# Root product moved into the maxima, transposes of a chunk issued earlier, ScalarE's register loads and two input loads moved

## What is computed

```python
h = maximum(layernorm(x), 0)
# layer 0: mean over incoming edges, applied twice
n1 = segment_sum(h[src], dst) / max(deg, 1)
n2 = segment_sum(n1[src], dst) / max(deg, 1)
x = x + 0.5 * n1 + 0.5 * n2
h = maximum(layernorm(x), 0)
# layer 1: two convolutions with a maximum over incoming edges
def conv(X, Wm, We, Wr, b):
    agg = segment_max(X[src] @ Wm + edge_attr @ We, dst)   # 0 where a node has no edge
    return agg + X @ Wr + b
c1 = leaky_relu(conv(h,  W1_msg, W1_edge, W1_root, b1))
c2 = leaky_relu(conv(c1, W2_msg, W2_edge, W2_root, b2))
return x + c2
```

## Time and profile before

| | us |
|---|---|
| median of 3 runs | 8090.3 (8090.01 to 8094.53) |
| profiled execution | 8085.28 |
| its span | 8083.5 |
| GpSimd busy (74%) | 5982.4 |
| TensorE busy (62%) | 5040.0 |
| VectorE busy (41%) | 3320.8 |
| ScalarE busy (18%) | 1432.1 |
| mean granted clock of TensorE | 0.700 of 2.4 GHz |

### The profile page before, as it was taken

How to read it: one execution, slowest core, us unless ns; L and a number is a source line. 1 busy time by engine, 2 the same in 40 slices (tenths; PEclk the granted TensorE clock), 3 DMA queues, 4 the chain that set the end, 5 groups by cost and what they waited for, 6 DMA issues and landing times.

```text
span 8083.5 us, 153739 instructions
## 1 busy us (share of the span) xinstructions
PE 5040.0 (62%) x25651; PEld 3760.0 (47%) x25651; DVE 3320.8 (41%) x7074; ACT 1432.1 (18%) x4686; POOL 5982.4 (74%) x6411
## 2 busy tenths in 40 slices
PE   3444454445344444444677878777787787878777
PEld 2333333334333333333555655555575565555556
DVE  5444444445433333333533433333343343333335
ACT  2000000001000000000422333323242232333323
POOL 6777777776777777777677777777766777777777
PEclk9965555556555555555677888888787888888888
DMA  3111111111211111111144444344323444444443
GB/s 92 42 42 41 42 41 41 41 41 47 57 41 42 41 41 41 41 41 41 40 94 93 98 92 97 89 96 93 92 69 91 98 93 92 98 93 92 95 95 80
DMA packets 337343, 553.28 MB, mean 68 GB/s; under 512 B 212648, under 2 KB 212648, under 8 KB 311848
## 3 DMA queue, kind: packets, MB, share of 16 engines
q0 software_dynamic: 196096, 301.60, 18.2%
q1 hardware_dynamic: 129796, 243.57, 11.8%
q10 hardware_dynamic: 10788, 2.16, 0.2%
HBM read 521.97 MB, written 24.87 MB: 68 GB/s over the span
## 4 chain that ended last, share of the span: by engine, by line
POOL 53%; issue 21%; SPq 10%; PE 10%; DMA 3%; DVE 2%; ACT 1%; ACTq 0%; DVEq 0%; POOLq 0%
POOL rows L443 53%; SPq L288 5%; SPq L311 4%; PE ps L673 3%; PE ps L671 3%; DMA rows<-table,src_sb 2%; PE ps L695 2%; SPq L294 1%; PE ps L684 1%; PE ps L757 1%; PE ps L770 1%; ACT arena L488 0%; DMA arena<-in_eat 0%; DMA table<-arena 0%; PE ps L652 0%
## 5 line engine op out<-in xcount | busy, mean ns | idle before, releaser
L443 POOL DMA_INDIRECT rows<-table,src_sb x6128 | 5788.3, 945 | 1957.9 <-issue 1847.0
L652 PE MATMUL ps<-arena,rows 128*98 128x128 f32 (+1 forms) x6088 | 1518.7, 430 | 2103.7 <-DMA rows<-table,src_sb 1362.9
L652 PEld LDWEIGHTS ps<-arena,rows 128*98 128x98 f32 (+1 forms) x6088 | 1263.9, 277 | 2381.1 <-DVE comp L882 2011.2
L897 DVE TENSOR_TENSOR_SCAN arena<-arena,ps 96x512 f32<-96x512 f32 x782 | 997.5, 1276 | 2424.3 <-PE ps L673 2419.5
L882 DVE TENSOR_TENSOR comp<-comp,ps 98x128 f32 (+1 forms) x3128 | 895.6, 286 | 2165.8 <-PE ps L652 1851.1
L671 PE MATMUL ps<-arena,we 32*96 32x512 f32 x1564 | 1001.2, 724 | 797.1 <-DMA rows<-table,src_sb 471.6
L673 PEld LDWEIGHTS ps<-ident,rows 128*96 128x96 f32 x6168 | 825.9, 188 | 718.8 <-issue 718.8
L865 DVE TENSOR_TENSOR arena<-ps,meta 128x512 f32<-128x512 f32 x1564 | 1051.0, 672 | 29.7 <-issue 26.1
L673 PE MATMUL ps<-ident,rows 128*96 128x128 f32 x6168 | 1017.0, 317 | 0.0
L513 ACT COPY comp<-ps 96x128 f32 x3128 | 818.9, 262 | 1067.2 <-PE ps L695 806.2
L695 PE MATMUL ps<-arena 128*96 128x128 f32 x6256 | 946.0, 302 | 1.3 <-ACT arena L504 1.3
(11 more groups left out here) (98 smaller groups left out, 1065.0 us busy)
## 6 DMA issues: line engine op xcount, KB each, us to landing
side<-table SPq DMA_DIRECT2D x10240, 0.4 KB
arena<-flags SPq DMA_DIRECT2D x194, 768.0 KB
rows<-table,src_sb POOLq DMA_INDIRECT x6128
side<-table ACTq DMA_DIRECT2D x5120, 0.4 KB
arena<-in_eat SPq DMA_DIRECT2D x194, 256.0 KB
table<-arena SPq DMA_DIRECT2D x56, 336.0 KB, 2.8
out<-xs SPq DMA_DIRECT2D x13, 336.0 KB
tail<-table SPq DMA_DIRECT2D x256, 0.4 KB
```

The lines of the kernel that those rows point to most:

```text
L443: pool.indirect_dma_start(rows[:, g % RING, j, 0:D], None, tables[r][:, :], bass.IndirectOffsetOnAxis(src_sb[:, c:c + 1], 0)).then_inc(lan ...
L652: m = pe.matmul(ps[0:w, at + k * P:at + (k + 1) * P], got[k][:, 0:w], hot[:, j % HOTS, k, :], start=True, stop=True)
L897: dve.tensor_tensor_scan(run[:, slot % SCANS], fe[0:D, slot // UNIT, q * W:(q + 1) * W], ps[0:D, ROWS + slot % 2 * BANK:ROWS + slot % 2 * ...
```

## The change

- In rounds 2 and 3 `own_part` is new on ScalarE and TensorE. In each sweep of 8 groups two tiles of `root`, which now holds the nodes' features themselves, are copied to `h_tile`, transposed, copied to `h_turned_sb` (its row 96 is ones), multiplied with the root weights and bias, and copied back over the tile in `root`.
- In rounds 1 and 2 the features go straight into `root` (L488 and L1050 write there), the product has 96 columns, and the copy L595 and the last chunk's second product L778 are gone. The ones row of `hT` and its memset are gone, and `iota_0`, which nothing read.
- PSUM of the spread in rounds 1 and 2 lies apart from the transposes; the wait for VectorE's read is now the spread's. In rounds 0 and 3 the transposes have two places in PSUM and the spread trails by two chunks on TensorE (`PE_LAG`). TensorE's node steps of rounds 1 and 2 are written out, without a loop.
- ScalarE's register loads stand at the head of a step, before the wait for the transposes.
- The sources are loaded after the store of chunk 1 instead of 8, the two destination arrays after the store of chunk 13.

The diff, cut to what acts:

```diff
-PREP_ALL = 17
-PREP_MAX = 21
+PREP_ALL = 18
+PREP_MAX = 22
+        h_tile, at = carve(at, [P, D])
-        hT, at = carve(at, [D + 1, 2, CHUNK * P], parts=D + 1)
+        hT, at = carve(at, [D, 2, CHUNK * P], parts=D)
+        h_turned_sb = sb("h_turned_sb", [D + 1, P])
-        SPREAD = {0: (4 * BANK, 6 * BANK), 1: (0, 0), 2: (0, 0), 3: (4 * BANK, 6 * BANK)}
+        SPREAD = {0: (4 * BANK, 6 * BANK), 1: (6 * BANK, 6 * BANK), 2: (6 * BANK, 6 * BANK), 3: (4 * BANK, 6 * BANK)}
+        TURN, PART = 5 * BANK, 5 * BANK + 256
+        TURNED = {r: ((0, 2 * BANK) if r in (0, 3) else (0, 0)) for r in range(ROUNDS)}
+        PE_LAG = {0: 2, 1: 0, 2: 0, 3: 2}
...
@@ sync
-                elif q == 8:
+                elif q == 1:
                     sp.dma_start(src_sb[:, :], srcs.bitcast(U32)).then_inc(s_src, 16)
-                elif q == 9:
-                    sp.dma_start(cur_i, cur).then_inc(s_dst, 16)
-                elif q == 10:
-                    sp.dma_start(prev_i, prev).then_inc(s_dst, 16)
+            sp.dma_start(cur_i, cur).then_inc(s_dst, 16)
+            sp.dma_start(prev_i, prev).then_inc(s_dst, 16)
...
-                sp.wait_ge(root_sb[r - 1], CHUNKS)
+                sp.wait_ge(prod[r - 1], CHUNKS)
...
@@ scalar, norm
+                    to = root[:, bass.ds(q * (CHUNK * D) + j * D, D)] if k else hbuf[:, s, j, :]
+                    m = act.activation(to, xs[:, bass.ds(q * (CHUNK * D) + j * D, D)], ACT.Relu,
@@ scalar
+                def own_part(i, j):
+                    past = (r - 2) * TILES + i * 2
+                    if j == 4 or j == 6:
+                        t = past + (j - 4) // 2
+                        if j == 4:
+                            act.wait_ge(h_ps, past + 2)
+                        act.wait_ge(root_ps, t + 1)
+                        act.sem_inc(act_go, 1)
+                        at = bass.ds(i * (2 * D) + (j - 4) // 2 * D, D)
+                        act.copy(root[:, at], ps[:, PART:PART + D]).then_inc(root_sb, 1)
+                    if j == 2 or j == 4:
+                        t = past + (j - 2) // 2
+                        act.wait_ge(h_ps, t + 1)
+                        act.copy(h_turned_sb[0:D, :], ps[0:D, TURN:TURN + P]).then_inc(h_sb, 1)
+                    if j == 0 or j == 2:
+                        t = past + j // 2
+                        if j or not known(i) or past:
+                            act.wait_ge(h_ps, t)
+                            act.sem_inc(act_go, 1)
+                        at = bass.ds(i * (2 * D) + j // 2 * D, D)
+                        act.copy(h_tile[:], root[:, at]).then_inc(h_staged, 1)
...
                         g = i * RING + j
+                        own_part(i, j)
                         if after(g, 1):
                             copy_running(g - 1, j - 1)
...
@@ scalar, nodes
+                    if not known(k) or k + ahead < CHUNKS:
+                        coming = starts_of(k + ahead)
                     if has(k, 0):
                         act.wait_ge(win_ps[r], k + 1)
...
-                        act.copy(chunk(root, q), rv).then_inc(root_sb[r], 1)
...
-                        windows_of(k + ahead, (s + ahead) % 2, starts_of(k + ahead))
+                        windows_of(k + ahead, (s + ahead) % 2, coming)
@@ tensor
+                def own_part(i, j):
+                    past = (r - 2) * TILES + i * 2
+                    if j == 3 or j == 5:
+                        t = past + (j - 3) // 2
+                        pe.wait_ge(h_sb, t + 1)
+                        if j == 5 or not known(i) or past:
+                            pe.wait_ge(root_sb, t)
+                        pe.matmul(ps[:, PART:PART + D], h_turned_sb[:, :], wcat[:, r - 2, D:2 * D],
+                                  start=True, stop=True).then_inc(root_ps, 1)
+                    if j == 1 or j == 3:
+                        t = past + (j - 1) // 2
+                        pe.wait_ge(h_staged, t + 1)
+                        if j == 1 and (not known(i) or past):
+                            pe.wait_ge(root_sb, t)
+                        pe.transpose(ps[0:D, TURN:TURN + P], h_tile[:, :], ident[:, :]).then_inc(h_ps, 1)
...
                         rows_of(i, g, j, seen, here)
+                        own_part(i, j)
                         if after(g, 1):
                             back(g - 1, j - 1)
...
@@ tensor, nodes
-                        if after(k, 1):
+                        if lag == 0 and after(k, 1):
                             pe.wait_ge(win_sb[r], k)
-                            if lag == 0:
-                                pe.wait_ge(stepA[r], (k - 1) * STEPS[r] + READ[r])
+                        elif lag and after(k, 2):
+                            pe.wait_ge(win_sb[r], k - 1)
...
+                        if lag == 0 and after(q, 1):
+                            pe.wait_ge(stepA[r], (q - 1) * STEPS[r] + READ[r])
                         at_spread = SPREAD[r][qs]
...
-                            pe.wait_ge(root_sb[r], q)
+                            pe.wait_ge(out_sb[r], q)
...
-                        cols = D if last else 2 * D
...
+                            m = pe.matmul(ps[:, PROD + j * P:PROD + j * P + D], hT[:, qs, j * P:(j + 1) * P],
+                                          wcat[0:D, r - 1, 0:D], start=True, stop=True)
...
+                if r in projected:
+                    for k in range(CHUNKS + LAGS[r]):
+                        nodes(k, k % 2)
+                else:
+                    pipeline(pe, nodes, max(LAGS[r], PE_LAG[r]))
@@ vector
+            step(dve.memset(h_turned_sb[D:D + 1], 1.0))
...
-                            dve.wait_ge(root_sb[r - 1], CHUNKS)
+                            dve.wait_ge(root_sb, (r - 1) * TILES)
...
+                        to = chunk(root, q) if r == 2 else hbuf[:, qs]
+                        a(dve.scalar_tensor_tensor(to, tmp[:], SLOPE, tmp[:], ALU.mult, ALU.max), 2)
```

More of the change, by code:

```diff
@@ L423, in _ @@
                                pattern=[[0, P]], channel_multiplier=1).then_inc(const, 1)
-            for to, w, step, first in ((iota_0, P, 1, 0), (iota_1, P, 1, 1), (iota_b, P, 1, 0), (tile_at, TILES, P, 0)):
+            for to, w, step, first in ((iota_1, P, 1, 1), (iota_b, P, 1, 0), (tile_at, TILES, P, 0)):
                 pool.iota(to[:], pattern=[[step, w]], base=first, channel_multiplier=0,
@@ L546, in _ @@
                 ahead = 1 if r == 1 else 2
+                if r == 1:
+                    act.wait_ge(s_flags, 16)
                 def starts_of(k):
@@ L581, in nodes @@
                         w = X if r == 0 else D
-                        act.copy(win_c[:, s, :, 0:w], ps[:, 0:CHUNK * P].rearrange("p (t c) -> p t c", c=P)[:, :, 0:w]
+                        act.copy(win_c[:, s, :, 0:w], ps[:, TURNED[r][s]:TURNED[r][s] + CHUNK * P].rearrange("p (t c) -> p t c", c=P)[:, :, 0:w]
                                  ).then_inc(win_sb[r], 1)
@@ L611, in _ @@
         def _(pe):
[L612 removed]
+            pe.wait_ge(const, 11)
             pe.wait_ge(prep, PREP_START)
@@ L744, in nodes @@
                         for j in range(CHUNK):
-                            m = pe.transpose(ps[0:D, TRANS + j * P:TRANS + (j + 1) * P], hbuf[:, qs, j, :], ident[:, :])
+                            m = pe.transpose(ps[0:D, TRANS + j * P:TRANS + (j + 1) * P], root[:, (q * CHUNK + j) * D:(q * CHUNK + j + 1) * D], ident[:, :])
                         m.then_inc(ht_ps[r], 1)
@@ L1045, in nodes @@
                         if not after(q, 1):
-                            dve.wait_ge(root_sb[r - 1], CHUNKS)
+                            dve.wait_ge(root_sb, (r - 1) * TILES)
                         a(dve.tensor_tensor(tmp[:], agg, chunk(root, q), ALU.add), 1)
-                        if r == 2 and after(q, 2):
-                            dve.wait_ge(ht_ps[2], q - 1)
-                        a(dve.scalar_tensor_tensor(hbuf[:, qs], tmp[:], SLOPE, tmp[:], ALU.mult, ALU.max), 2)
+                        to = chunk(root, q) if r == 2 else hbuf[:, qs]
+                        a(dve.scalar_tensor_tensor(to, tmp[:], SLOPE, tmp[:], ALU.mult, ALU.max), 2)
                         if r == 3:
```

40 lines of the change are left out of this document (11 added, 29 removed).

## The result

The changed kernel takes 8075.65 us (median of 22 runs, 8068.28 to 8080.62), the kernel before in the same runs 8091.92 (8083.5 to 8098.18): a ratio of 0.998, interval 0.9975 to 0.9986. The profiled execution took 8077.61 us, its span is 8075.9. Forecast were 8077.5 and a range of 8067 to 8088.

The account below looks back on a forecast made before the run. GpSimd's indirect DMA issue bounds the four gathers, so only the 429 us outside could shrink. Terms -10.7, -7.7, +2.3, +1.6, +1.4 and +0.3 sum to -12.8: 8090.3 becomes 8077.5 us, range 8067 to 8088.

Parts of the forecast that it names:

- a GpSimd wait for TensorE of more than 0.5 us: Sign that the prediction is wrong: gathers 2 and 3 were to stay at 1,924.8 us without such a wait.
- Node stage 2: Round 2's node stage: shorter periods 7.3 us, drain 1.3, start 2.6 less 0.5; together -10.7 us, bounds 8 and 12.5.
- the chain from rel tile through one-hots to spread: Round 2's node stage: ScalarE's staging, GpSimd's one-hots, then TensorE's spread were to limit the period at 4.9 us.
- Node stage 1: Round 1's node stage: ten chunks save 5.7 us, first three 1.6, drain 0.4; together -7.7, bounds 4 and 10.5.
- the loop of 11.4 us for two chunks: Round 1's node stage: rel tile through aggregate and deviation to the rel tile after next, 5.7 us a chunk.
- The last stage: Round 3's nodes and output: VectorE-bound, with a later start from loads and transposes further ahead; +2.3 us, bounds 0 to 3.
- Node stage 0: Round 0's nodes: later start, less than round 3's since the first spread waited for one-hots anyhow; +1.6 us, bounds 0 to 2.5.
- Prologue and gather 0: Moved loads: stores -2.1 us, sources +0.8, GpSimd issues stretched under VectorE's preparation +2.7; together +1.4, bounds minus 2 to plus 4.
- Root product in the maxima: Gathers 2 and 3: the work fits beside GpSimd's issue, one or two side groups could touch; +0.3 us, bounds 0 and 4.
- rival (c): Maxima: TensorE waits for ScalarE, is late at ten side groups, GpSimd stalls on its ring; +17 us, 8094; chance 0.06.
- Moving the loads: Round 1's node stage: register loads, seven gaps of 6.3 us in all, were to run under the normalising activations.
- rival (d): Moving the loads does nothing, round 1 keeps its gaps; 2 us less gain, 8080; inside the forecast, no chance of its own.

Follow-up runs that it names:

- no_own: Changed kernel without the root product in the maxima, so the output lacks the root part; 8074.2 us, ratio 0.998 to the kernel before.
- product3: Changed kernel with TensorE making three of the seven products of every chunk of rounds 1 and 2 twice; 12568.8 us, ratio 0.993 to the kernel before.
- psum_back: Changed kernel with transposes and spread of rounds 1 and 2 in one PSUM place again; 8077.9 us, ratio 0.9983 to the kernel before.
- copy2: Changed kernel with ScalarE copying every chunk's product out of PSUM twice in rounds 1 and 2; 12582.1 us, ratio 0.9931 to the kernel before.
- before_second: The kernel before, unedited, profiled once more; 12574.6 us, ratio 1.0017 to the kernel before.
- loads_back: Changed kernel with ScalarE's register loads right ahead of the window copies again, behind the rel tile; 8095.5 us, ratio 1.0006 to the kernel before.
- the second group: The runs lag1_second, psum_back, loads_back and no_own, each one edit to the changed kernel; 8070.95, 8077.9, 8095.5 and 8074.2 us.
- lag1_second: Changed kernel with the transposes of rounds 0 and 3 only one chunk ahead of their spreads again; 8070.95 us, ratio 0.9973 to the kernel before.
- again: The changed kernel, unedited, profiled once more; 12585.9 us, ratio 0.9931 to the kernel before.
- rows_early: Changed kernel with SyncE's side rows of rounds 2 and 3 spread over the first sixteen units of a batch; 12402.6 us, ratio 0.9877 to the kernel before.

## Why the prediction was right, and which terms were off

The forecast was -12.8 us and the medians say -16.3. The two places where time was to be won, the steady parts of node stages 1 and 2, are as forecast: 5.85 and 4.9 us a chunk forecast, 5.77 and 4.76 to 4.78 measured. That the sum came out so near is in part luck, for errors of 2 to 5 us in single terms stand against each other. One of the prediction's own signs of being wrong did show, a GpSimd wait for TensorE of more than 0.5 us (2.61, in gather 2); no_own has such waits as well.

**Node stage 2, forecast -10.7, measured -13.9.** The period: forecast 4.9, bound by the chain from rel tile through one-hots to spread; measured 4.76 to 4.78, and what TensorE does sets it (product3). The product gave back 0.74 us, not 0.67, and the chain from rel tile to spread takes 4.31 us where I had 4.44 and is just not late; 1.2 us over ten chunks. The start: 2.6 less 0.5 forecast, 7.4 less 0.8 measured (the first three chunks, and the first spread later behind its rel tile). I counted the wait for VectorE's read and the shorter product, and left out the clock, which rose sooner in every profile without that wait; 2.8 of the 7.4 are left when the PSUM place is taken back, and no run divides them further. In the first three chunks the granted clock was 0.58 in psum_back, and 0.54 before and 0.70 after (us, PE busy, clock, DMA share, GB/s):

```profile
5991.15:6013.45 22.30, 19.34 (x91) 0.54 0.00 1
```

```profile
5994.04:6008.95 14.91, 14.01 (x92) 0.70 0.01 2
```

Against this stands a drain 2.7 us longer in this execution.

**Node stage 1, -7.7 against -5.5.** The period is right (5.85 forecast, 5.77 measured; ten of them save 6.7 us where 5.7 were forecast), and so is ScalarE's 5.45 (copy2). That the loop of 11.4 us for two chunks is what stands above it was not tested; product3 shows only that it isn't TensorE. Wrong is the drain: -0.4 forecast, +1.5 measured, 20.3 to 20.8 us in all ten profiles whose products are as changed and hold no added work, 18.9 and 19.4 before. TensorE has less to do at the end. Its clock falls at 4033.4, 13.8 us before the end, and stays at 1.2 GHz (13.7 to 14.4 us before the end in all ten), where before it rose again at 4035.4 for 10 us (here) or fell 7.5 us before the end (before_second). A product of half the columns then takes 3.30 us; that the smaller work is what brings the fall is inferred from these profiles:

```profile
4033.54 3.30 PE L818 MATMUL ps<-wcat,arena 96*128 96x96 f32 x14 [1.70 <-DVE arena L1043]
```

The first three chunks' 1.6 didn't show in this profile (0.2), but with 18.6 to 23.6 in all kernels they are not a term that one execution can tell.

**The last stage, +2.3 against +6.9.** The mechanism and its size (2.2) are as forecast. The rest is the drain of gather 3, 16.9 us here and 12.9 before, and 0.8 in the first three chunks. TensorE's clock in it, of the changed kernel and of loads_back (drain 11.3):

```profile
7996.80:8008.80 12.00, 12.00 (x49) 9.54 (x49) 3.71 (x4) 2.14 (x7) 0.04 (x1) 0.50 0.02 5
```

```profile
8014.00:8025.30 11.30, 8.75 (x66) 6.76 (x64) 3.92 (x5) 6.42 (x24) 0.00 (x0) 1.00 0.03 5
```

At 1.2 GHz TensorE is busy for all 12 us, at 2.4 GHz it has gaps. The clock is not all of it: psum_back's drain took 13.9 us at 2.4 GHz. What decides the level an execution gets there was not found. The prediction had no term for the two drains, +2.7 and +4.0 in this pair of profiles. In the five profiles after the change (this one and the second group) the drain before node stage 2 takes 11.4 to 16.9 us, against 10.8 in the one before, and that of gather 3 11.3 to 16.9 against 12.9; how much of them belongs to the change is open.

**Node stage 0, +1.6 against +2.0.** Right number, wrong step, and so luck: the forecast put all of it before VectorE's first step, which came 0.6 us later, and to the lead, which costs nothing here (lag1_second, 70.4). The other 1.5 are in the ten periods (35.9 against 34.5), of which the kernel before shows 1.1 too when profiled again.

**Prologue and gather 0, +1.4 against +0.7.** Gather 0 with its stretched issues is +2.7 (forecast 2.7), the prologue -1.9 here and about -1 on the average (forecast -1.3). "SBUF — State Buffer" of the Trainium skill, section on who interferes with whom, puts such stretching on VectorE's copies and scalar operations in their two-port modes, and infers that a two-input operation, which contends with GpSimd's reads, leaves the writing of descriptors alone; the trace disagrees with the inference as far as an indirect DMA goes, whose row numbers also stand in SBUF. Beside two steps with two SBUF inputs each and nothing else of VectorE's an issue takes 1.74 us instead of 0.945, here in again:

```profile
84.68 1.78 DVE L981 TENSOR_TENSOR root<-root 128x1564 f32<-128x1564 int32 x1
85.54 1.74 POOL L449 DMA_INDIRECT rows<-table,src_sb  x1 [0.30 <-issue]
86.49 1.79 DVE L982 TENSOR_TENSOR root<-root 128x1564 f32<-128x1564 f32 x1
```

The longest, 2.53 us at 62.70, stands beside both kinds: a TENSOR_TENSOR until 64.10 and a CAST until 65.1.

**Root product in the maxima, +0.3 against +2.4.** no_own shows that the work costs nothing that can be told. The GpSimd waits at side groups, rival (c)'s mechanism, occur without it; where they come from is the order of SyncE's rows (rows_early), and whether the change made them more frequent is open.

**Moving the loads.** I priced it at the 6.3 us of gaps that the trace of before showed, and called doing nothing rival (d). loads_back is 20 us slower than the changed kernel. For the case that the move does nothing (d) had 8080 us; without the move it is 8095.5, 15 us more. The total was right because the change holds both halves: the prediction priced the gaps and not what they do to TensorE's clock.

## What to carry to other kernels

Price an edit against the order it leaves behind, not against the trace of before: the same register loads in the same place went with ten periods of 64.4 us in one order and of 78.4 us in another. An instruction taken away may have been the cover of the next wait (here, it is argued, a copy of 0.61 us over a register load of 1.0 to 2.2). Where TensorE comes to wait in the middle of a stage, look at its granted clock first, for it can cost more than the wait (16.5 of 20.7 us here). A register load belongs ahead of long work on its own engine and never right behind an instruction that waits. And a stage that begins or ends with a thin TensorE differs by 5 to 6 us between executions of the same code, so compare the steady part and the ends apart, each over several profiles.

## What the hardware showed

- A row fetched by a plain DMA took SyncE 0.58 us in one group of runs and about 1.9 in two others, ScalarE 0.61 and about 1.5, for the same instructions, but in those two only while GpSimd issued indirect DMAs. In again SyncE took 1.88 us a row from 300 to 500 us, with 134 issues of GpSimd in that time, and 0.58 from 600 to 720, with none; in the kernel before 0.60 and 0.57, with 161 and 96 issues. Over the whole of again some 5,100 rows with GpSimd issuing took 1.52 us on the average and as many without 0.60. In the trace single sequencer steps of 29 to 37 ns then take about 700 ns again and again. Why it is so in some groups and not in others was not found; indirect DMAs (0.945 and 0.947 us) and engine operations kept their durations.
- ScalarE's sequencer goes on to a register load while earlier operations run, but not past an operation that still waits (begun at 4007.97, behind a deviation that had waited until 4007.71); in node stage 1 the load takes 1.0 to 2.4 us.
- With less work for TensorE at the end of a stage each remaining matmul was slower, in ten profiles of ten: fourteen of 96 columns took 1.73 us at the high level of the clock and 3.30 at the low one. In the middle of a stage (loads_back, round 1) waits of up to 1.7 us went with a granted clock of 0.74 instead of 0.98.
